# Decoder layer on one core: the cross attention's context rows and Wk Wq prepared inside the MLP, the last chunk turned back first, router biases loaded earlier

## The chip, the core and the metric

The kernel runs on one core of a Trainium2 chip. TensorE (PE) does the matmuls, VectorE (DVE), ScalarE (ACT) and GpSimd (POOL) the element-wise work, SyncE (SP) issues most DMAs. Each engine works through a queue of its own in program order; engines wait for each other by semaphores. The metric is the device time of one execution in microseconds (us), lower is better.

## What is computed

One decoder layer on 2048 tokens of 256 columns, in float32, each part with a residual and a layer norm. Cut to what matters here:

```python
x = layernorm(x + attn(x))            # decayed linear attention, then an MLP 256 -> 1024 -> 256
x = layernorm(x + xattn(x, context))  # context: 1601 rows of 256
x = layernorm(x + ffn(x))             # 8 experts, top 2

def xattn(slots, P, ...):
    Pn = rmsnorm(P, input_norm_w)
    k_proj, v_proj = Pn @ Wk.T, Pn @ Wv.T
    for _ in range(3):
        sn = rmsnorm(slots, slot_norm_w)
        scores = (sn @ Wq.T) @ k_proj.T * d ** -0.5
        attn = softmax(scores, axis=-2)                  # over the slots
        attn = attn / (sum(attn, axis=-1) + eps)
        slots = gru(attn @ v_proj, slots)

def ffn(x):                                              # router
    logits = x @ router_w + router_b + expert_bias
    # softmax, top 2, each token through its two experts
```

## The kernel before

The layer is a sequence of blocks; between two blocks all engines meet. Tokens are worked in NC = 4 chunks of CH = 512 columns, or NT = 16 tiles of P = 128 rows (TPC = 4 tiles in a chunk); the context in MT = 13 row tiles, the last with 65 rows. A column of 256 is DH = 2 halves. Products that need float32 accuracy are made from two parts each, a high part rounded to the fast format (`_hi`, a copy by ACT or POOL) and the rest (`_lo`, a subtraction by DVE or POOL), in three matmuls (`three_pass`, lines 74 to 78).

**`decay_attention_and_mlp`** makes the attention and the MLP, and ends with the layer norm of its result, turned into `sT` (columns on partitions). In the MLP loop over chunks c, PE makes 8 up-products of f (bank 6 or 7), ACT takes GELU (line 330) and its high part (335), DVE the low part `g_lo` (488); then PE makes the down-products of the chunk's 4 tiles, DVE adds them to the residual and normalises them (lines 496 to 505), and PE turns the normalised chunk (`turn_x1`, 588), which ACT copies to `sT` (`take_x1`, 306). ACT's GELU n waits until DVE has made the low part of n - 2 (`g_ok`); PE's up-product n waits for GELU n - 2 (`gelu_ok`). DVE's queue holds for each chunk: 8 low parts, 4 tiles, a chain of small operations (`rsqrt_steps`, 63 to 71, each waiting for the one before), 4 scalings; then the next chunk's low parts. POOL's residual additions (247, 248) lie in the MLP's first chunk. In the tail PE turns chunks 2 and 3. SP loads at the start, among others, `wk`, `wq`, `wv`, the turned context `cxT` and the norm weights (`early`), and stores each finished chunk.

**`prepare_context`** is a block of its own. Its work:

- PE makes Wk Wq (bank 0 and 1), which DVE scales to `wkq`; two broadcasts of the slots' norm factors (`norm.broadcast`); 8 key products (`keys`, 1450: wkq by cxT, 6 of 512 columns and 2 of 65), the other two broadcasts among them; and then `wi` = Wv by the GRU's weights (1457).
- ACT makes the high parts of the slots (`slots_hi`, 703), of the keys (1352), keeps the broadcasts in `rsB` (779), makes the context rows' 13 sums of squares (1364), and the high parts of `wh` (1373), of the context rows (1376, in two groups of 8 and 5 tiles) and of `wi` (1379).
- DVE makes the diagonals for the broadcasts (699), low parts of slots (707) and keys (1397), then waits for the 13 sums of squares, makes the rows' factors by the small chain, scales the 13 row tiles (1416), and makes the low parts of the rows' first group (1421) and of `wi` (1424), and the biases (1428 to 1430).
- POOL makes the low parts of `wh` (1337) and of the rows' second group (1339).
- SP loads the context rows `cx` (1.6 MB) and the GRU's weights when the block begins.

**`cross_attention`** then runs three iterations. In each, PE makes score products (m, c) of context tile m and slot chunk c; DVE scales each by `rsB` (1003, `scale(m, c)`); ACT takes the exponential; PE multiplies the weights by the rows; and a GRU updates the slots by chunk. At the end of an iteration SP writes the norm factors of chunks 0 to 2 to memory and loads them back spread over the partitions into `rsB` (`rs_in`); the last chunk's factors go another way (square sums by PE at 734, the chain by DVE from 742, a broadcast by PE). The first scaling of the next iteration, scale(0, 0), waits for all three loads. PE's order there: (0,0), (0,1), (0,2), (1,0), (1,1), square sums, (1,2), (0,3), broadcast. DVE's: scale(0,0), (0,1), low part of the last slots, scale(0,2), (1,0), the chain, and on. POOL adds the squares of the last chunk.

Behind the third iteration each chunk is turned back to rows (`turn_back`, 1161), added to the residual by DVE (955), normalised (`factors_of` by DVE, `apply` by ACT at 858), turned again (`turn_rows`, 1173) and multiplied by the router (`logits`, 1181); DVE takes the logits (`take_logits`, 965).

**`route`** loads the two bias vectors, adds them to the logits (1592, 1593), and finds for each token its experts and places. POOL makes constants meanwhile. SP loads, behind the biases, the experts' biases and 8 MB of `w2`. **`experts`** begins when those have landed: ACT's first high parts of `w1` (1794), DVE's low parts (1845), then the turned tokens (1839), then PE's first product.

## Time and profile before

| | |
|---|---|
| runs of the kernel | 1331.2, 1335.5, 1340.9 us; median 1335.5 |
| the profiled execution | 1336.2 us, of which the profile's span is 1334.4 |
| mean granted TensorE clock | 0.936 of 2.4 GHz |
| PE, DVE, ACT, POOL busy, share of the span | 88%, 66%, 47%, 19% |
| MLP (from its first up-product) | 90.6 to 203.0 us |
| preparation of the context | 210.4 to 248.2 us |
| three iterations | 248.7 to 946.8 us |
| last norm, router, experts, combination | 946.8 to 1334.4 us |

How to read the rows: in a timeline a row gives the start in us from the span's start, the duration in us, the engine, the line of the kernel, the operation, the tiles (out<-in), shapes and how many are merged. In brackets stands how long the engine had been idle before, and what ended the idle time. A group by line gives after the bar busy us and mean ns of one, then the idle time before them. PE is TensorE's matmuls, PEld its weight loads, SPq the DMA issues of SyncE. `x_psum`, `a_psum` are the PSUM banks. A table of stretches gives for each the length, then busy us of PE, PEld, DVE, ACT, POOL with the number of instructions in brackets, the granted clock as a share of 2.4 GHz, the DMA share and GB/s.

### The profile page before, as it was taken

How to read it: one execution, taken by the hardware profiler on the slowest of the kernel's cores; microseconds unless marked ns; L12 is line 12 of the kernel's file. 1: busy time of each engine (PE TensorE's matmuls, PEld its weight loads, DVE VectorE, ACT ScalarE, POOL GpSimd, SP SyncE). 2: the span in 40 equal slices, each digit the busy share in tenths (PEclk: the TensorE clock that was granted, in tenths of full speed). 3: DMA queues.
4: the chain of work that ended last, by engine and by line, in shares of the span. 5: the costliest groups of instructions: out<-in, count | busy, mean ns of one | idle time of the engine just before them, and what ended most of it. 6: DMA issues, size and time to landing. Idle time of an engine off the chain costs nothing. (4 is left out here: it accounts for less than half of the span.)

```text
span 1334.4 us, 18897 instructions
## 1 busy us (share of the span) xinstructions
PE 1176.1 (88%) x6332; PEld 981.9 (74%) x6332; DVE 884.1 (66%) x1863; ACT 621.1 (47%) x1057; POOL 251.2 (19%) x317
## 2 busy tenths in 40 slices
PE   6968997699999989999998999999628999999950
PEld 5437894478787867878786787778528999999950
DVE  4646545698745669874556987456466777777747
ACT  4335535354434334443433445334206777777733
POOL 3016000200000000000000000000035666666623
PEclk8869998899999999999999999999758999999985
DMA  7000003000010000001000000270081111111143
GB/s 275 1 0 10 23 17 112 1 0 1 0 28 5 17 9 0 1 0 32 1 17 9 0 1 0 63 285 32 32 285 41 46 38 43 47 43 43 40 150 126
DMA packets 43566, 62.57 MB, mean 47 GB/s; under 512 B 13102, under 2 KB 33264, under 8 KB 42608
## 3 DMA queue, kind: packets, MB, share of 16 engines
q1 hardware_dynamic: 37856, 47.35, 10.5%
q0 software_dynamic: 4416, 12.06, 3.0%
q10 hardware_dynamic: 1232, 2.36, 0.5%
q8 instruction: 36, 0.59, 0.2%
q14 instruction: 26, 0.21, 0.1%
HBM read 49.40 MB, written 12.36 MB: 46 GB/s over the span
## 5 line engine op out<-in xcount | busy, mean ns | idle before, releaser
L76 PE MATMUL x_psum<-x_sn_lo,x_kq_hi 128*128 128x512 f32 (+1 forms) x312 | 126.5, 405 | 17.8 <-PEq L1324 12.0
L76 PE MATMUL x_psum<-x_p_lo,x_v_hi 128*128 128x512 f32 (+1 forms) x312 | 125.9, 404 | 5.2 <-DVE x_p_lo L990 5.2
L77 PE MATMUL x_psum<-x_sn_hi,x_kq_lo 128*128 128x512 f32 (+1 forms) x312 | 124.8, 400 | 0.0
L78 PE MATMUL x_psum<-x_sn_hi,x_kq_hi 128*128 128x512 f32 (+1 forms) x312 | 124.4, 399 | 0.0
L77 PE MATMUL x_psum<-x_p_hi,x_v_lo 128*128 128x512 f32 (+1 forms) x312 | 123.0, 394 | 0.0
L78 PE MATMUL x_psum<-x_p_hi,x_v_hi 128*128 128x512 f32 (+1 forms) x312 | 123.0, 394 | 0.0
L899 ACT ACTIVATE x_e<-x_e,x_inv 128x1024 f32<-128x1024 f32 (+1 forms) x39 | 45.0, 1153 | 142.0 <-DVE x_inv L1009 142.0
L76 PE MATMUL e_bank<-e_w_lo,e_g_hi 128*128 128x256 f32 x368 | 107.6, 292 | 0.1
L76 PE MATMUL e_bank<-e_xT_lo,e_w_hi 128*128 128x256 f32 x368 | 105.1, 286 | 2.1 <-DVE e_xT_lo L1839 1.4
L78 PE MATMUL e_bank<-e_xT_hi,e_w_hi 128*128 128x256 f32 x368 | 104.8, 285 | 0.0
L77 PE MATMUL e_bank<-e_xT_hi,e_w_lo 128*128 128x256 f32 x368 | 104.8, 285 | 0.0
L77 PE MATMUL e_bank<-e_w_hi,e_g_lo 128*128 128x256 f32 x368 | 103.9, 282 | 0.0
L78 PE MATMUL e_bank<-e_w_hi,e_g_hi 128*128 128x256 f32 x368 | 103.8, 282 | 0.0
L726 POOL TENSOR_TENSOR x_E_rest<-x_E_rest 128x512 f32<-128x512 f32 x8 | 10.4, 1296 | 454.0 <-ACT x_E_rest L720 454.0
L1809 ACT ACTIVATE sT<-e_bank,b 128x256 f32<-128x256 f32 x184 | 76.9, 469 | 19.2 <-PE e_bank L78 19.2
L76 PEld LDWEIGHTS x_psum<-x_sn_lo,x_kq_hi 128*128 128x128 f32 (+1 forms) x312 | 58.6, 188 | 35.4 <-issue 12.4
L1853 DVE TENSOR_TENSOR e_w_lo<-w,e_w_hi 128x512 fp32r<-128x512 f32 x92 | 66.0, 718 | 27.4 <-issue 14.3
L1865 DVE TENSOR_TENSOR e_g_lo<-sT,e_g_hi 128x512 fp32r<-128x512 f32 x92 | 63.7, 692 | 28.1 <-ACT e_g_hi L1814 19.6
L76 PEld LDWEIGHTS x_psum<-x_p_lo,x_v_hi 128*128 128x128 f32 (+1 forms) x312 | 58.6, 188 | 24.3 <-DVE x_p_lo L990 9.4
L76 PEld LDWEIGHTS e_bank<-e_xT_lo,e_w_hi 128*128 128x128 f32 x368 | 71.4, 194 | 2.7 <-DVE e_xT_lo L1839 1.8
L76 PEld LDWEIGHTS e_bank<-e_w_lo,e_g_hi 128*128 128x128 f32 x368 | 70.1, 191 | 2.7 <-DVE e_w_lo L1853 0.4
L77 PEld LDWEIGHTS e_bank<-e_xT_hi,e_w_lo 128*128 128x128 f32 x368 | 71.4, 194 | 0.0
(392 smaller groups left out, 3132.3 us busy)
## 6 DMA issues: line engine op xcount, KB each, us to landing
w<-in_w SPq DMA_DIRECT2D x16, 1024.0 KB, 12.6
w<-scratch_results SPq DMA_DIRECT2D x8, 512.0 KB, 8.0
x_E_first<-scratch_row_inv SPq DMA_DIRECT2D x3, 1024.0 KB, 4.7
sT<-in_xT ACTq DMA_DIRECT2D x4, 512.0 KB, 12.4
a_x<-in_x SPq DMA_DIRECT2D x4, 512.0 KB, 8.3
scratch_x<-a_h SPq DMA_DIRECT2D x4, 512.0 KB, 2.7
w<-scratch_x SPq DMA_DIRECT2D x1, 2048.0 KB, 8.2
out<-w SPq DMA_DIRECT2D x4, 512.0 KB, 2.9
```

Source lines behind the costliest of these rows:

```text
L76: pe.matmul(out, w_hi, x_lo, start=start, stop=False)
L77: pe.matmul(out, w_lo, x_hi, start=False, stop=False)
L78: return pe.matmul(out, w_hi, x_hi, start=False, stop=stop)
L726: pool.tensor_tensor(sq[:, 0], sq[:, 0], sq[:, 1], ALU.add).then_inc(sum_ok, 1)
L899: act.activation(scores, scores, ACT.Exp, bias=inv[0:n, m, 0:1], accum_out=mx[0:n, m % 2, NC + half:NC + half + 1]).then_inc(exp_ok, 1)
L1809: act.activation(g32[f % 2][:, a], bank[1 + f % 2][:, a * SLOTS:(a + 1) * SLOTS], ACT.Gelu, bias=b1[:, bass.ds(ex * FT + (2 * f + a), 1)]) ...
L1853: v.tensor_tensor(w2_lo[:, 2 * f:2 * f + 2], w2[:, bass.ds(ex, 1), 2 * f:2 * f + 2].rearrange("p e c f -> p (e c) f"), w2_hi[:, 2 * f:2 * ...
L1865: v.tensor_tensor(g_lo[:, 2 * f:2 * f + 2], g32[f % 2], g_hi[:, 2 * f:2 * f + 2].bitcast(F32), ALU.subtract).then_inc(g_lo_ok, 1)
```

## The change

- The context rows, `wkq` and the rows' factors get places that lie in the MLP's memory, over buffers of the attention that are free by then. SP loads the rows once the attention's result `h2` is complete and POOL has cleared the last tile.
- ACT makes the 13 sums of squares behind chunk 1's last GELU; DVE makes the factors and scales the rows in place behind chunk 1's layer norm, ahead of chunk 2's low parts.
- PE makes Wk Wq between `turn_x1(2)` and `turn_x1(3)`; ACT, not DVE, scales it, between the two `take_x1`.
- In the preparation PE begins with a key product and puts the broadcasts between the first keys; ACT's and DVE's orders are written anew (the rows' high parts early, the last two keys late); POOL splits the rows before `wh`; the biases are made before the low part of `wi`; SP loads only the GRU's weights.
- In the iterations the first scaling waits for two slices of `rsB`; the third has a semaphore of its own, for which scale(0, 2) waits.
- `turn_back(3)` comes before `turn_rows(2)` and `logits(2)`.
- The router's two bias vectors are loaded at the start of the cross attention; `router_b` is added by `take_logits`, and `route` begins with one addition less and without its wait.

```diff
@@ decay_attention_and_mlp
+        context_at = -(-nc.sbuf_base // 32) * 32
+        for name, shape in (("cx", [P, MT, D]), ("wkq", [P, DH, D]), ("c_ss", [P, MT]), ("c_rs", [P, MT]), ("c_tmp", [P, MT])):
+            early[name] = nc.alloc_sbuf_tensor_at("y_" + name, shape, F32, offset=context_at)
+            context_at = -(-(context_at + math.prod(shape[1:]) * 4) // 32) * 32
...
+            sp.wait_ge(cx_zeroed, 1)
+            sp.dma_start(cx[:, 0:FULL], io["ctx"][0:FULL * P].rearrange("(t p) d -> p t d", p=P)).then_inc(ld_cx, 16)
+            sp.dma_start(cx[0:MROWS[-1], FULL], io["ctx"][FULL * P:]).then_inc(ld_cx, 16)
...
             pool.wait_ge(h2_sb, 2 * NC)
+            pool.memset(cx[:, FULL], 0.0).then_inc(cx_zeroed, 1)
             pool.wait_ge(up_mm, 2)
...
+                if c == 1:
+                    act.wait_ge(ld_cx, 32)
+                    for m in range(MT):
+                        if m >= 2:
+                            act.wait_ge(cx_squares, m - 1)
+                        act.activation(junk[:, m % 2], cx[:, m], ACT.Square, accum_out=c_ss[:, m:m + 1]).then_inc(cx_squares, 1)
             take_x1(NC - 2)
+            for h in range(DH):
+                act.wait_ge(wkq_mm, h + 1)
+                act.activation(wkq[:, h], bank[6 + h][:, 0:D], ACT.Copy, scale=early["cols"][:, h:h + 1])
             take_x1(NC - 1)
...
                 last.then_inc(x1_ok, 1)
+                if c == 1:
+                    v.wait_ge(cx_squares, MT)
+                    k.step(v.tensor_scalar(c_ss[:], c_ss[:], 1.0 / D, EPS_RMS, ALU.mult, ALU.add))
+                    rsqrt_steps(v, k, c_rs[:], c_ss[:], c_tmp[:])
+                    for m in range(MT):
+                        v.tensor_scalar(cx[:, m], cx[:, m], c_rs[:, m:m + 1], None, ALU.mult)
...
             turn_x1(NC - 2)
+            pe.wait_ge(gelu_ok, NC * FT)
+            pe.wait_ge(shared["ld_early"], 80)
+            for h in range(DH):
+                for j in range(DH):
+                    last = pe.matmul(bank[6 + h][:, 0:D], early["wk"][:, j, h * P:(h + 1) * P], early["wq"][:, j],
+                                     start=(j == 0), stop=(j == DH - 1))
+                last.then_inc(wkq_mm, 1)
             turn_x1(NC - 1)
@@ cross_attention
-                v.tensor_copy(shared["lg"][:, c * TPC:(c + 1) * TPC], bank[7][:, 0:TPC * NE].rearrange("p (t e) -> p t e", e=NE)).then_inc(lg_ok, 1)
+                v.tensor_tensor(shared["lg"][:, c * TPC:(c + 1) * TPC], bank[7][:, 0:TPC * NE].rearrange("p (t e) -> p t e", e=NE),
+                                bc(rb[:, 0], 1, TPC), ALU.add).then_inc(lg_ok, 1)
...
                     if c == 0 and m == 0 and it > 0:
-                        v.wait_ge(rs_in, 16 * it * (NC - 1))
+                        v.wait_ge(rs_in, 16 * it * 2)
+                    if c == 2 and m == 0 and it > 0:
+                        v.wait_ge(rs_last_in, 16 * it)
...
+            sp.dma_start(rb[:, 0], io["router_b"].partition_broadcast(P)).then_inc(ld_r, 16)
+            sp.dma_start(rb[:, 1], io["expert_bias"].partition_broadcast(P)).then_inc(ld_r, 16)
...
+            turn_back(NC - 1)
             turn_rows(NC - 2)
             logits(NC - 2)
-            turn_back(NC - 1)
             turn_rows(NC - 1)
             logits(NC - 1)
@@ prepare_context: POOL
+            pool.wait_ge(v_hi_ok, 2)
+            pool.tensor_tensor(v_lo[:, VG[1]], v32[:, VG[1]], v_hi[:, VG[1]].bitcast(F32), ALU.subtract).then_inc(wh_lo_ok, 1)
             pool.wait_ge(wh_hi_ok, 1)
             pool.tensor_tensor(wh_lo[:], whT[:], wh_hi[:].bitcast(F32), ALU.subtract).then_inc(wh_lo_ok, 1)
-            pool.wait_ge(v_hi_ok, 2)
-            pool.tensor_tensor(v_lo[:, VG[1]], v32[:, VG[1]], v_hi[:, VG[1]].bitcast(F32), ALU.subtract).then_inc(wh_lo_ok, 1)
@@ prepare_context: ACT (order after)
+            slots_hi(act, 0)
             keys_hi(0)
             norm.keep(act, 0, 0)
+            slots_hi(act, 1)
             keys_hi(1)
             norm.keep(act, 1, 1)
+            keys_hi(2)
+            keys_hi(3)
             slots_hi(act, 2)
             norm.keep(act, 2, 2)
+            rows_hi(0)
+            keys_hi(4)
+            keys_hi(5)
             slots_hi(act, 3)
             norm.keep(act, 3, 3)
+            rows_hi(1)
             act.wait_ge(ld_g, 48)
             act.activation(wh_hi[:], whT[:], ACT.Copy).then_inc(wh_hi_ok, 1)
+            for i in range(6, len(keys)):
+                keys_hi(i)
@@ prepare_context: DVE
-            v.memset(cx[:, FULL], 0.0).then_inc(zeroed, 1)
             norm.spread(v, slot_rs, 0, 0)
             norm.spread(v, slot_rs, 1, 1)
-            v.wait_ge(ld_early, 80)
-            for h in range(DH):
-                v.wait_ge(wkq_mm, h + 1)
-                v.tensor_scalar(wkq[:, h], bank[h][:, 0:D], cols[:, h:h + 1], None, ALU.mult).then_inc(wkq_ok, 1)
+            k.mark(v.tensor_scalar(rs16[:], rs[:], float(D) ** -0.5, None, ALU.mult))
...
+            keys_lo(3)
             slots_lo(v, 2, 2)
-            keys_lo(3)
+            keys_lo(4)
+            keys_lo(5)
             slots_lo(v, 3, 3)
-            v.wait_ge(squares, MT)
-            k.step(v.tensor_scalar(ss[:], ss[:], 1.0 / D, EPS_RMS, ALU.mult, ALU.add))
-            rsqrt_steps(v, k, rs[:], ss[:], tmp[:])
-            for m in range(MT):
-                v.tensor_scalar(v32[:, m], cx[:, m], rs[:, m:m + 1], None, ALU.mult).then_inc(v32_ok, 1)
-            k.step(v.tensor_scalar(rs16[:], rs[:], float(D) ** -0.5, None, ALU.mult))
...
+            v.wait_ge(ld_g, 48)
+            k.mark(v.tensor_tensor(bias[:, 0:2 * DH], bi[:, 0:2 * DH], bi[:, 3 * DH:5 * DH], ALU.add))
@@ prepare_context: PE
-            norm.broadcast(pe, 0, 0)
-            norm.broadcast(pe, 1, 1)
-            pe.wait_ge(wkq_ok, DH)
             for i, (h, c) in enumerate(keys):
-                if i == 4 or i == 6:
-                    norm.broadcast(pe, i // 2, i // 2)
+                if i in (1, 2, 4, 6):
+                    g = (1, 2, 4, 6).index(i)
+                    norm.broadcast(pe, g, g)
@@ route
-            sp.dma_start(rb[:, 0], io["router_b"].partition_broadcast(P)).then_inc(ld_r, 16)
-            sp.dma_start(rb[:, 1], io["expert_bias"].partition_broadcast(P)).then_inc(ld_r, 16)
...
-            v.wait_ge(ld_r, 32)
-            k.step(v.tensor_tensor(lg[:], lg[:], bc(rb[:, 0], 1, NT), ALU.add))
             k.step(v.tensor_tensor(lg[:], lg[:], bc(rb[:, 1], 1, NT), ALU.add))
```

## Rows read from the trace of the kernel before

**Rows 1.** The page's first part: an engine's busy us, share of the span, instructions

```profile
PE 1176.1 (88%) x6332; PEld 981.9 (74%) x6332; DVE 884.1 (66%) x1863; ACT 621.1 (47%) x1057; POOL 251.2 (19%) x317
```

**Rows 2.** Timeline, edge of MLP chunks 1 and 2: start, us, engine, line, operation

```profile
154.36 0.69 ACT L330 ACTIVATE a_g<-a_psum,a_small 128x512 f32<-128x512 f32 x1 [12.15 <-PE a_psum L78]
...
157.85 1.29 DVE L488 TENSOR_TENSOR a_g_lo<-a_g,a_g_hi 128x512 fp32r<-128x512 f32 x2
...
158.63 0.69 ACT L330 ACTIVATE a_g<-a_psum,a_small 128x512 f32<-128x512 f32 x1 [1.56 <-DVE a_g_lo L488]
...
159.37 0.50 PE L76 MATMUL a_psum<-a_hT_lo,a_w_hi 128*128 128x512 f32 x1 [0.97 <-ACT a_g L330]
```

**Rows 3.** Groups by line, 208 to 260 us: busy us, mean ns of one, idle before

```profile
L1364 ACT ACTIVATE y_junk<-y_cx 128x256 f32<-128x256 f32 x13 | 5.2, 409 | 0.0
...
L1339 POOL TENSOR_TENSOR x_v_lo<-y_v,x_v_hi 128x1280 fp32r<-128x1280 f32 x1 | 3.8, 3835 | 7.0 <-ACT x_v_hi L1376 7.0
...
L1416 DVE TENSOR_SCALAR y_v<-y_cx,y_rs 128x256 f32<-128x256 f32 x13 | 3.5, 344 | 0.0
...
L1337 POOL TENSOR_TENSOR x_wh_lo<-y_whT,x_wh_hi 128x1536 fp32r<-128x1536 f32 x1 | 3.4, 3424 | 110.4 <-ACT x_wh_hi L1373 110.4
...
L1421 DVE TENSOR_TENSOR x_v_lo<-y_v,x_v_hi 128x2048 fp32r<-128x2048 f32 x1 | 2.3, 2292 | 0.1
...
L1424 DVE SCALAR_TENSOR_TENSOR x_wi_lo<-x_psum,y_cols,x_wi_hi 128x512 fp32r<-128x512 f32 (+1 forms) x4 | 2.2, 610 | 0.0
```

**Rows 4.** Busy us by stretch: PE, PEld, DVE, ACT, POOL, granted clock, DMA, GB/s

```profile
210.40:248.50 38.10, 24.21 (x64) 12.81 (x64) 27.38 (x65) 21.54 (x49) 7.26 (x2) 0.86 0.25 85
...
248.50:252.00 3.50, 3.25 (x8) 2.60 (x9) 0.53 (x2) 1.28 (x1) 0.00 (x0) 0.50 0.07 9
...
482.00:484.00 2.00, 2.00 (x6) 1.58 (x5) 1.57 (x5) 0.00 (x0) 0.00 (x0) 0.50 0.03 8
```

**Rows 5.** Timeline of DVE in the preparation

```profile
231.85 0.16 DVE L1413 TENSOR_SCALAR y_ss<-y_ss 128x13 f32<-128x13 f32 x1
...
233.92 3.37 DVE L70 TENSOR_TENSOR y_tmp<-y_tmp,y_ss 128x13 f32<-128x13 f32 x1
...
248.07 0.15 DVE L1430 COPY x_bias<-y_bi 128x2 f32<-128x2 f32 x1
```

**Rows 6.** Timeline of PE, end of the MLP and preparation

```profile
207.24 1.59 PE L588 MATMUL a_psum<-ident,a_h 128*128 128x128 f32 x8 [4.27 <-DVE a_h L505]
...
215.94 7.03 PE L1450 MATMUL x_psum<-y_cxT,y_wkq 128*128 128x512 f32 x16
```

**Rows 7.** Timeline of ACT, DVE and PE at the start of the second iteration

```profile
478.67 1.04 ACT L703 ACTIVATE x_sn_hi<-sT 128x1024 fp32r<-128x1024 f32 x1
...
479.58 0.75 DVE L1003 CUSTOM_DVE_ANT_0 x_e<-x_psum,x_rsB,x_rs 128x512 f32<-128x512 f32 x1 [1.91 <-DMA x_rsB<-scratch_slot_inv]
...
480.39 0.56 PE L76 MATMUL x_psum<-x_sn_lo,x_kq_hi 128*128 128x512 f32 x1 [2.23 <-DVE x_mx L1003]
...
485.82 0.16 DVE L742 TENSOR_SCALAR x_st<-x_psum 128x4 f32<-128x4 f32 x1 [1.94 <-PE x_psum L734]
```

**Rows 8.** Timeline of DVE and PE behind the last iteration

```profile
946.10 0.69 DVE L1102 TENSOR_TENSOR sT<-sT,x_E_rest 128x512 f32<-128x512 f32 x1
...
946.94 1.06 PE L1173 MATMUL x_psum<-ident,x_acc 128*128 128x128 f32 x8 [3.88 <-ACT x_acc L858]
...
953.38 1.48 DVE L955 TENSOR_TENSOR x_acc<-x_psum,x_acc 128x512 f32<-128x512 f32 x2 [6.59 <-PE x_psum L1161]
```

**Rows 9.** Timeline, routing and start of the experts

```profile
969.07 0.42 SPq L1553 DMA_DIRECT2D b<-in_b_cols  x1
...
971.17 0.29 DVE L1592 TENSOR_TENSOR lg<-lg,r_rb 128x128 f32<-128x128 f32 x1 [3.26 <-DMA r_rb<-in_expert_bias]
...
1000.97 1.15 ACT L1794 ACTIVATE e_w_hi<-w 128x512 fp32r x2 [28.19 <-DMA w<-in_w]
...
1006.28 0.58 PE L76 MATMUL e_bank<-e_xT_lo,e_w_hi 128*128 128x256 f32 x1 [1.41 <-DVE e_xT_lo L1839]
```

78 lines of the change are left out of this document (27 added, 51 removed).

## The prediction

> **What bounds the kernel now.** I read the page first: PE is busy 88% of the span, so a microsecond that PE loses is lost unless another engine had been late anyway, and what can be gained lies in the stretches where PE waits [rows 1]. The page's chain of the work that ended last covers only the last 40 us, so I went to the timeline of each engine around every edit, and to the clock and busy time by stretch.
>
> In the MLP, PE runs from chunk to chunk almost without a gap. The reader is to see what the gap of 0.97 us at 159.37 hangs on: PE's fifth up-product of chunk 2 waits for ACT's third GELU (158.63), and that waits for DVE's first `g_lo` of the chunk (157.85), which stands in DVE's queue behind the layer norm of chunk 1. ACT, in contrast, had been idle 12.15 us before its first GELU of the chunk [rows 2]. So at the edge between two chunks DVE has no slack at all and ACT has a lot.
>
> The preparation of the context runs from 210.4 to the end of the DVE copies at 248.22: 37.8 us. PE works 24.2 of it, DVE 27.4, ACT 21.5 [rows 4, 5]. The end is DVE's: it waits for its own square sums, scales 13 row tiles, and only then come the split of the rows and of `wi`.
>
> **The change, part by part** (plus is slower).
>
> *Squares and loading in the MLP.* ACT's 13 squares cost 5.2 us [rows 3] and come behind chunk 1's last GELU, in the 12.15 us of idle: 7 us stay, so zero. The context rows are asked for once `h2` is complete, before the first up-product, and are needed two chunks of products later; SP's next job, the first x1 store, is much later too, and POOL's memset stands in front of a wait for PE: zero.
>
> *Scaling in the MLP.* DVE gets 12 small chained operations and 13 scalings right behind the norm of chunk 1, ahead of the first `g_lo` of chunk 2. The small ones follow each other every 0.207 us (ten from 231.85 to 233.92), so 12 cost 2.5 us [rows 5]; the 13 scalings cost 3.5 [rows 3]. The `g_lo` at 157.85 comes 6.0 us later, the GELU too, and PE stands from 158.40 to about 165.3: +6.0, nothing hides it, since PE could already run only four up-products ahead. After such a pause PE's clock is low: in the first 3.5 us after the pause before 248.5 the granted clock is 0.50, which is 1.2 GHz of 2.4 [rows 4], and those 3.5 us do 1.75 us of work. I take +1.7 (bounds 0 and 2). PE then bounds the chunk again, so it is not won back. Together **+7.7** (6.0 to 8.0).
>
> *Wk Wq in the MLP's tail.* The eight instructions of 256 columns cost 1.7 us at the rate of the keys (16 of 512 in 7.03), 3.4 at the low clock, and PE is idle 4.27 us there, before it turns the last chunk at 207.24 [rows 6]; ACT's two copies also lie there. Zero; without this cover at most what runs over, under 1 us.
>
> *The preparation.* Gone are the Wk Wq products and DVE's two scalings of them, the squares, the chain and the row scalings. I laid the new order out from the block's start B, each step as long as its row of before. PE: a key product of four instructions takes 1.7 us at the full clock (16 in 7.03, four keys) [rows 6], twice that in the first 3.5 us; with the four broadcasts the sixth key is ready at B+14.6. ACT: high halves of slots and keys, copies and the two high halves of the rows follow one another and end at B+18.4; `wh_hi` ends at B+19.8, the last two keys at B+20.4. ACT's total work of 21.5 minus the squares [rows 3, 4] says the same from the other side: 16.3 less the 2 for `wi_hi` is 14.3, and it waits about 5 for its first keys. PE has the `wi` products (8 of 512 columns and 8 of 256, 5.3 at the same rate) done by B+22.6. What is late next is DVE and POOL. POOL splits its rows from B+18.4: 1280 columns at the rate of its 1536 in 3.42 [rows 3] are 2.85, to B+21.3. Then DVE's 2.13 (2.29 [rows 3], less the overlap) and POOL's 3.4 for `wh_lo` are both ready. They exclude each other: in before, a DVE operation of 13 columns took 3.37 us at 233.92, exactly while POOL was splitting `wh` [rows 5]; and POOL's own 1280 columns took 3.84 instead of 2.85 beside DVE's split [rows 3]. So they queue, in either order: B+21.3 + 2.1 + 3.4 = B+26.8, and then DVE's bias operations (0.6, the first has two SBUF inputs and queues too) and `wi_lo` (2.2 [rows 3]): B+29.5. Against 37.8 that is **-8.3**. If they never met the end would be B+25.5, gain 12.3; if the order of ACT costs two further microseconds the gain is 6.
>
> The Trainium skill (SBUF — State Buffer, section "SBUF: two separate sides") says that a DVE instruction with two SBUF inputs and a GpSimd instruction that reads SBUF take the shared ports as a lock, for the whole instruction. The trace agrees (3.37 us for 13 columns). By it DVE and POOL queue in the new order; with no such rule the total would be some 4 us lower.
>
> *The split wait at an iteration's start.* DVE's first scaling waits 1.91 us for the third slice of `rsB`, until 479.58, and PE 2.23 behind it [rows 7]; PE even falls to the low clock (0.50 from 482 to 484 [rows 4]). The new wait needs two slices, long there. The third is needed by scale(0, 2), which comes after two scalings (0.67 each from 477.67) and the low half of the last slots, which needs ACT's high half of 478.67 to 479.71: 480.9, past the landing at 479.6. So no new wait. PE runs products (1, 0) and (1, 1) from 478.4 instead of 480.39, 2.0 earlier, at full clock, which is 1.4 more; the square sums reach DVE at 482.3 instead of 485.82 [rows 7]: -3.5. There are two such boundaries: **-7.0**. Bounds: the waits alone, -3.8 (if PE's clock falls all the same), and somewhat more than 7 where the slice lands later, since all of the wait goes.
>
> *Last chunk turned back first.* Before, PE's order was rows of chunk 2, logits of chunk 2 and only then the last chunk; DVE was idle 6.59 us until 953.38. The slots are ready when DVE ends at 946.8, and PE starts 8 transposes in 1.06 us at 946.94 [rows 8]. In the new order these are the last chunk's: DVE starts at 947.5. Everything to the end of this stage hangs on that norm: **-5.9** (bounds: 5.2, if half of a low clock is met there, and the idle 6.59). Chunk 2's rows and logits move back 1.1 us and end by 954, before ACT has applied the last norm: zero.
>
> *Router biases.* DVE no longer waits 3.26 us and has one addition less (0.3), but POOL's constants bind it again after 2.7. Routing ends 2.7 earlier. The experts however start when the last expert weights land, 1000.97; ACT waited 28.19 for them [rows 9]. SP's first job behind the two bias loads is at 969.07, so that without them it is some 0.9 earlier (DVE had ended the stage before at 967.9), and DVE's four splits of `w1` then stand ahead of `xT_lo`, which lay before 1006.28 with ACT's copy still 1.3 behind; this queue allows 2.1. **-1.9** (bounds 0, if the gather lands no sooner, and -2.7). The two loads go to SP's queue at the start of the iterations, ahead of a wait for the first iteration's row sums: zero.
>
> The Trainium skill (DMA: Bandwidth & Descriptors, section "Queues, rings and completion order") has each DMA engine take turns between its queues, packet by packet. No row shows gather and weights together. By that rule an earlier gather shares with the weights and is not stuck behind them; if it were stuck, the gain would be the 0.9 alone.
>
> Sum: +7.7 - 8.3 - 7.0 - 5.9 - 1.9 = -15.4. The profiled execution took 1336.2 (span 1334.4 and 1.8 around it): 1320.8. The median of the runs is 0.7 below it: I predict **1320**.
>
> **Rivals.**
> 1. *Small gains.* PE's clock falls at both boundaries (-3.8), the preparation gains 6, the router nothing or 0.9: +8 - 6 - 3.8 - 5.2 - 0.5 = -7.5, 1328. For it: a pause of 2.2 us sufficed for the low clock at 480 [rows 4, 7], and a pause of about 1.9 remains ahead of the broadcast. Against it: there the square sums still come 2 us earlier.
> 2. *DVE and POOL do not meet, or the block opens at full clock*: 12.3 from the preparation, +6.5 in the MLP: -20.6, 1315. For it: the tail of the MLP now has PE work in its pause. Against: 3.37 us at 233.92 [rows 5].
> 3. *Slower.* PE does not get its full clock back after the 6.9 us pause in chunk 2. From 159.37 to the pause that ends at 207.24 [rows 2, 6] there are 42.6 us of dense work; all of it at 1.2 GHz costs 42.6 more in the place of 1.7: +25.5, 1361. It decides from 58 us of time at the low level (29 us lost: 15.4 eaten up, 13.4 to pass 1%). Against: after 248.5 the low level lasted 3.5 us [rows 4].
> 4. *The change does not do what it says*: the context rows land late and ACT's squares hold its GELUs. They have two chunks of products to land 1.6 MB; I give it nothing of its own.
>
> **How the numbers follow.** Forecast 0.50, rival 1 0.28, rival 2 0.18, rival 3 0.04. The forecast's own range, from its bounds, is 1316 to 1325. To leave out no more than 2 in 10 the range takes in rival 1 and most of rival 2: 1313 to 1329. A measurement of this kernel tells about 1% from no change, 13.4 us, so 1322.1 is the line. Of the forecast 0.44 lies below it, and all of rival 2; of rival 1 nothing: faster 0.62. Slower by over 1% is rival 3: 0.04. The rest, 0.34, is within 1%.
>
> **What would show it.** In chunk 2 of the MLP one PE wait for ACT of 6.9 us in the place of 0.97, with the clock at 0.50 behind it; a preparation of 29.5 us with DVE's split or POOL's visibly stretched; no DMA wait of DVE at the first scaling, and the square sums 3.5 us earlier; DVE's wait for the turned last chunk below 1 us; a wait for the weights still ahead of the experts. I am wrong in the sum if DVE's insertion costs PE less than 5 (some slack I don't see), or if the preparation ends in ACT rather than in DVE and POOL.

## The result, and the profile after

| | before | changed |
|---|---|---|
| median of 12 runs | 1333.8 us (1331.2 to 1341.9) | 1324.9 us (1321.4 to 1330.0) |
| the profiled execution, and its span | 1336.2, 1334.4 us | 1321.4, 1319.7 us |
| PE busy | 1176.1 us | 1176.3 us |

The ratio is 0.9927 with a 95% interval of 0.9903 to 0.9951: 9.7 us less (6.5 to 12.9). The time lies in the range, and even at the edge of the forecast's own range (1316 to 1325); the gain however was forecast as 15.4 us, and 62% of the chance had been put on a gain of over 1%, which this isn't.

The spans of the two profiled executions stand 14.7 us apart, more than the medians (8.9). So the first thing to do is to cut both into stages at points that both traces have: first up-product of the MLP; first high part of the slots (ACT); first score product; the last GRU addition of each iteration (DVE); DVE's last take of the logits; first expert product. Each stage is the difference of two starts.

| stage, us | before | changed | difference | forecast |
|---|---|---|---|---|
| attention (untouched) | 90.6 | 86.1 | -4.5 | 0 |
| MLP | 119.8 | 127.3 | +7.5 | +7.7 |
| preparation | 38.3 | 30.7 | -7.6 | -8.3 |
| first iteration | 228.2 | 230.7 | +2.4 | 0 |
| second and third | 469.1 | 463.8 | -5.3 | -7.0 |
| last norm | 21.6 | 16.4 | -5.2 | -5.9 |
| routing | 38.6 | 36.4 | -2.1 | -1.9 |
| experts (untouched) | 328.1 | 328.2 | +0.1 | 0 |

The attention has the same code in both, and its 4.5 us are PE's clock alone: the granted clock falls there at other moments. Over the 14 profiled kernels of this study the attention takes 86.0 to 95.7 us. Without the two untouched stages the change is worth -10.3 in this pair of traces, which agrees with the ratio of the runs.

**MLP.** Timeline of DVE, ACT and PE in the changed kernel, where [rows 2] showed the edge between chunks 1 and 2: start, us, engine, line, operation, and in brackets the idle time and what ended it.

```profile
152.88 0.17 DVE L529 TENSOR_SCALAR y_c_ss<-y_c_ss 128x13 f32<-128x13 f32 x1
...
155.38 3.50 DVE L532 TENSOR_SCALAR y_cx<-y_cx,y_c_rs 128x256 f32<-128x256 f32 x13
158.80 1.28 DVE L508 TENSOR_TENSOR a_g_lo<-a_g,a_g_hi 128x512 fp32r<-128x512 f32 x2
...
159.57 0.69 ACT L341 ACTIVATE a_g<-a_psum,a_small 128x512 f32<-128x512 f32 x1 [7.47 <-DVE a_g_lo L508]
...
160.31 0.79 PE L76 MATMUL a_psum<-a_hT_lo,a_w_hi 128*128 128x512 f32 x1 [6.88 <-ACT a_g L341]
```

The chain and the 13 scalings fill DVE from 152.88 to 158.8, the third GELU waits for the low part behind them, and PE stands 6.88 us in the place of 0.97.

**Preparation.** Timeline of DVE and POOL, the counterpart of [rows 5].

```profile
233.01 2.90 POOL L1366 TENSOR_TENSOR x_v_lo<-y_cx,x_v_hi 128x1280 fp32r<-128x1280 f32 x1 [114.48 <-ACT x_v_hi L1381]
...
234.95 3.10 DVE L1439 TENSOR_TENSOR x_v_lo<-y_cx,x_v_hi 128x2048 fp32r<-128x2048 f32 x1
...
235.87 5.46 POOL L1368 TENSOR_TENSOR x_wh_lo<-y_whT,x_wh_hi 128x1536 fp32r<-128x1536 f32 x1
...
237.98 3.37 DVE L1441 TENSOR_TENSOR x_bias<-y_bi 128x4 f32<-128x4 f32 x1
...
241.41 2.18 DVE L1446 SCALAR_TENSOR_TENSOR x_wi_lo<-x_psum,y_cols,x_wi_hi 128x512 fp32r<-128x512 f32 x4
```

POOL's split of 1280 columns ends at 235.91, and DVE's of 2048, begun at 234.95, takes 3.10 us instead of 2.29 in before [rows 3]. Then POOL takes 5.46 us for what took 3.42, the rest of DVE's split (235.9 to 238.0) and then its own 3.4 us, and DVE's addition of four columns takes 3.37 us, to 241.35, just past the end of POOL's split at 241.33. So each of the two engines in turn is stretched to the other's end, three times in a row, and `wi_lo` comes last.

**Clock.** Busy us of PE, PEld, DVE, ACT, POOL by stretch, then the granted clock, the DMA share and GB/s, the counterpart of [rows 4].

```profile
213.40:244.00 30.60, 23.15 (x56) 11.08 (x56) 21.60 (x37) 16.82 (x23) 8.32 (x2) 0.83 0.14 52
244.10:247.60 3.50, 3.47 (x8) 2.81 (x9) 0.76 (x2) 1.28 (x1) 0.00 (x0) 0.50 0.11 12
247.60:249.60 2.00, 2.00 (x6) 1.53 (x5) 0.23 (x2) 0.00 (x0) 0.00 (x0) 0.50 0.00 0
485.60:488.60 3.00, 3.00 (x9) 2.32 (x8) 1.40 (x5) 2.97 (x4) 0.00 (x0) 0.50 0.00 0
```

Behind the first score product (244.13) the clock is at 0.50 (1.2 GHz) until 250.1, that is for 6.0 us, where it had been 3.2 in before (248.75 to 252.0). It is at 0.50 once more behind the boundary between two iterations, now from 485.6, behind the broadcast; there it lasts 3.4 us. Such a stretch at 0.50 in the middle of PE's work is called a low spell from here on.

**Boundary, last norm, routing.** Timeline of DVE, PE and ACT, the counterpart of [rows 7 to 9].

```profile
475.42 0.74 DVE L1040 CUSTOM_DVE_ANT_0 x_e<-x_psum,x_rsB,x_rs 128x512 f32<-128x512 f32 x1
...
480.32 0.15 DVE L775 TENSOR_SCALAR x_st<-x_psum 128x4 f32<-128x4 f32 x1
...
484.80 0.50 PE L807 MATMUL x_psum<-x_diag_parts,x_ones_r 128*128 128x512 f32 x1 [1.87 <-DVE x_diag_parts L792]
...
939.54 1.90 PE L1200 MATMUL x_psum<-ident,sT 128*128 128x128 f32 x8 [3.99 <-DVE sT L1139]
...
940.69 1.48 DVE L989 TENSOR_TENSOR x_acc<-x_psum,x_acc 128x512 f32<-128x512 f32 x2 [1.41 <-PE x_psum L1200]
...
955.04 0.19 DVE L999 TENSOR_TENSOR lg<-x_psum,rb 128x32 f32<-128x32 f32 x1 [8.34 <-PE x_psum L1220]
955.55 0.29 DVE L1599 TENSOR_TENSOR lg<-lg,rb 128x128 f32<-128x128 f32 x1 [0.32 <-PEq L683]
...
984.83 2.19 ACT L1800 ACTIVATE e_w_hi<-w 128x512 fp32r x4 [27.62 <-DMA w<-in_w]
...
988.96 1.12 PE L1902 MATMUL e_bank<-ident,sT 128*128 128x128 f32 x4 [7.90 <-DMA sT<-scratch_x,e_tokens]
991.49 0.58 PE L76 MATMUL e_bank<-e_xT_lo,e_w_hi 128*128 128x256 f32 x1 [1.41 <-DVE e_xT_lo L1845]
```

The first scaling (475.42) has no wait. The square sums (480.32) come 5.51 us behind the last addition of the slots, 8.84 in before. The last chunk is turned first, and DVE waits 1.41 us for it instead of 6.59. Routing starts 0.3 us after its block, and the wait that ends last ahead of the experts is PE's for the gathered tokens (988.96); the weights have been there since 984.83. The last of the eight weight loads lands 28.9 us behind DVE's last take, and the gather's first DMA is issued at 29.1, so that whether the two share the DMA engines, as the prediction assumes, stays open.

### The profile page after: what moved, and what is told of

Read it like the earlier page. It is cut to its first block and busy times, and to the rows that moved or that the text cites. A ratio compares the mean times of both kernels' runs of the same rounds, so it can differ in the third digit from the quotient of the medians.

```text
span 1319.7 us, 18896 instructions
## 1 busy us (share of the span) xinstructions
PE 1176.3 (89%) x6332; PEld 983.3 (75%) x6332; DVE 883.1 (67%) x1859; ACT 622.7 (47%) x1059; POOL 253.2 (19%) x318
## 3 DMA queue, kind: packets, MB, share of 16 engines
q1 hardware_dynamic: 37856, 47.35, 10.3%
```

## The experiments

All stages of all kernels, in us, one profile each; the ratio is to the kernel before, of the timed ones. The first part undoes or isolates parts of the change, the second alters one thing in the changed kernel, the third combines what gained.

| kernel | attn | MLP | prep | it. 1 | it. 2 | it. 3 | norm | route | ratio (95%) |
|---|---|---|---|---|---|---|---|---|---|
| before | 90.6 | 119.8 | 38.3 | 228.2 | 232.3 | 236.8 | 21.6 | 38.6 | |
| changed | 86.1 | 127.3 | 30.7 | 230.7 | 229.0 | 234.8 | 16.4 | 36.4 | 0.9927 (0.9903, 0.9951) |
| p_late | 86.0 | 119.3 | 38.1 | 228.1 | 229.5 | 232.7 | 15.8 | 36.2 | 0.9918 (0.9886, 0.9951) |
| p_early | 86.0 | 127.2 | 30.7 | 230.7 | 232.0 | 237.5 | 21.6 | 38.7 | 1.0022 (0.9991, 1.0053) |
| u_one_wait | 86.3 | 127.6 | 30.8 | 231.1 | 232.1 | 237.4 | 15.8 | 36.0 | |
| u_back_last | 86.0 | 127.3 | 30.7 | 230.7 | 229.0 | 234.3 | 21.9 | 35.9 | |
| u_router | 86.4 | 127.3 | 30.7 | 231.0 | 229.0 | 234.3 | 16.3 | 38.6 | |
| e_spread | 95.7 | 119.2 | 29.6 | 229.5 | 229.5 | 236.0 | 16.5 | 36.2 | 0.983 (0.979, 0.9869) |
| e_bias_last | 86.7 | 127.3 | 28.6 | 229.9 | 229.0 | 232.8 | 16.5 | 36.3 | 0.9897 (0.9849, 0.9946) |
| e_warm | 87.3 | 127.4 | 30.7 | 227.7 | 229.5 | 232.8 | 15.8 | 36.1 | |
| e_warm_tail | 87.6 | 128.9 | 27.7 | 229.9 | 229.0 | 234.3 | 16.4 | 36.2 | |
| e_warm_bound | 90.7 | 127.5 | 30.8 | 230.7 | 228.7 | 233.9 | 15.8 | 36.2 | |
| c_spread_bias | 90.6 | 119.6 | 27.7 | 228.9 | 229.0 | 233.7 | 15.9 | 36.4 | 0.98 (0.976, 0.9841) |
| c_all | 91.2 | 119.6 | 25.7 | 226.9 | 227.5 | 234.3 | 15.8 | 36.2 | 0.9782 (0.9748, 0.9817) |

### The two halves of the change: p_late and p_early

p_late is the kernel before with the split wait, `turn_back(NC - 1)` first and the router biases; p_early is the changed kernel with these three undone.

> The kernel before with only the three late parts of the change (the split wait for rsB, the last chunk turned back first, the router biases); the MLP and the preparation are those of before. Theory A (the stages of the two profiles add up): these parts account for -3.3 and -2.0 at the two boundaries, -5.2 behind the third iteration and -2.1 in routing, together -12.6 us, and the early half of the change is worth about nothing (+7.5 in the MLP, -7.6 in the preparation), so this kernel stands at 0.9905 of before and at or somewhat below the whole change. Theory B (the early half brings a gain that the late parts need, for example because the clock is better when the iterations begin earlier): it stands at 0.995 or above. The MLP's first pause in chunk 2 is 0.97 us again, the preparation 38.3 us.

> The whole change without its three late parts: only the context rows and Wk Wq in the MLP and the new order of the preparation. Theory A: +7.5 in the MLP and -7.6 in the preparation, and 0 to +2.5 in the first iteration if its longer low clock belongs to the change: within 0 to +2.5 us of before, ratio 0.999 to 1.002. Theory B (the early half is a gain of its own): ratio 0.997 or below. The profile shows the pause of 6.9 us in chunk 2 and a preparation of 30.7 us, and whether PE's clock stays low for 3.3 us after the first score product, as in before, or 5.2, as in the changed kernel.

Measured: 0.9918 and 1.0022. Theory A holds: p_early's interval leaves out theory B's 0.997, and p_late's only just reaches its 0.995. The product of the two is 0.9940, the whole change 0.9927. More than half of the diff, all that moves work into the MLP, brings nothing that can be measured: what the preparation gets back (-7.6) the MLP has paid (+7.5), and the first iteration takes 2.4 more on top.

### Each late part undone: u_one_wait, u_back_last, u_router

```diff
@@ u_one_wait
-                        v.wait_ge(rs_in, 16 * it * 2)
-                    if c == 2 and m == 0 and it > 0:
-                        v.wait_ge(rs_last_in, 16 * it)
+                        v.wait_ge(rs_in, 16 * it * (NC - 1))
...
@@ u_back_last
-            turn_back(NC - 1)
             turn_rows(NC - 2)
             logits(NC - 2)
+            turn_back(NC - 1)
@@ u_router: SP and DVE in routing; the two loads and the addition are gone from the cross attention
+            sp.dma_start(rb[:, 0], io["router_b"].partition_broadcast(P)).then_inc(ld_r, 16)
+            sp.dma_start(rb[:, 1], io["expert_bias"].partition_broadcast(P)).then_inc(ld_r, 16)
...
+            v.wait_ge(ld_r, 32)
+            k.step(v.tensor_tensor(lg[:], lg[:], bc(rb[:, 0], 1, NT), ALU.add))
```

> The changed kernel with one wait for all three slices of rsB again. Theory A (the gain at a boundary is the DMA wait alone, 1.9 to 2.3 us, since a low spell of PE's clock is paid either way): the square sums reach DVE 8.8 and 9.1 us after the last addition instead of 5.5, a low spell stands at the wait instead of behind the broadcast, and the second iteration takes 231 us, the third 236 to 237. A further low spell about 150 us behind the boundary (634 and 632 us in the two kernels with one wait so far, and in one of seven with the split wait) would add 1.7: 232.3. Theory B (the split saves the spell too, 3.5 at each boundary): 232.5 and 238.3.

Timeline of DVE in u_one_wait, the scaling and the square sums:

```profile
478.76 0.75 DVE L1038 CUSTOM_DVE_ANT_0 x_e<-x_psum,x_rsB,x_rs 128x512 f32<-128x512 f32 x1 [2.27 <-DMA x_rsB<-scratch_slot_inv]
...
484.91 0.16 DVE L775 TENSOR_SCALAR x_st<-x_psum 128x4 f32<-128x4 f32 x1 [1.61 <-PE x_psum L767]
```

The wait is back with 2.27 us, and the square sums come 9.11 us behind the last addition (475.80) instead of 5.5. The second and the third iteration take 232.1 and 237.4 us, 3.1 more each than in u_router, which has the split wait. Theory A had 232.3 for the second with a further low spell, and one stands at 633 us; theory B's 232.5 is too near to that to tell them apart. The third, 237.4, lies between A's 237 and B's 238.3, with a further spell at 865.

What tells them apart is a comparison at equal spells. The third iteration with a spell at the boundary and one late in the iteration takes 237.5 and 237.4 us with one wait (p_early, u_one_wait) and 236.0 with the split (e_spread); with the boundary's spell alone 236.8 (before) and 234.3 to 234.8 (changed, u_back_last, u_router, e_warm_tail). So the split is worth 1.4 to 2.5 us at this boundary, which is about the wait (2.27 us there in before), as in theory A. But a spell is not paid either way: the one-wait kernels have one at each of their 6 boundaries, the nine kernels with the split and no small products there at 14 of 18.

Over all kernels the second and third iteration together take 469.1, 469.4 and 469.5 us with one wait (before, p_early, u_one_wait) and 461.8 to 465.5, in the middle 463.3, with the split wait (those nine). That is 6.1 us, not 7.0. But the one-wait kernels have 3, 4 and 4 low spells in these two iterations and the nine others 1 to 3, 1.8 on average. At 1.7 us for a spell (half of 3.4) fewer spells make some 3 of the 6.1 us, by estimate, and the waits the other half.

> The changed kernel with the last chunk turned back behind the rows and logits of chunk 2 again. Expected by the stages: 21.6 us from the last addition to the last logits instead of 15.8 to 16.5, DVE's wait for the turned chunk 6.6 us instead of 1.4; routing unchanged at 36.2. If the order gained only what the clock gave (a rival reading of 16.5 against 15.8), less than 1 us.

Timeline of DVE in u_back_last: the residual addition behind the turned last chunk.

```profile
945.41 1.48 DVE L989 TENSOR_TENSOR x_acc<-x_psum,x_acc 128x512 f32<-128x512 f32 x2 [6.81 <-PE x_psum L1200]
```

As expected: 21.9 us and 6.81 us of wait. The order is worth 5.2 to 6.0 us (21.6 or 21.9 against 16.4 or 15.8).

> The changed kernel with the router's biases loaded and added in routing again. Theory A (routing is bound by the weights' landing in before and by the gather in the changed kernel): from the last logits to the first expert product 38.6 us instead of 36.2 to 36.4, the first low parts of w1 and the turned tokens next to each other as in before. Theory B (POOL's constants bind routing's start in both): DVE's first comparison waits the same 3.3 us but the stage is below 37. The last norm's stage stays at 16.5 or lower.

Timeline of DVE, ACT and PE in u_router: first addition, first high part of `w1`, turned tokens, first product.

```profile
958.49 0.29 DVE L1599 TENSOR_TENSOR lg<-lg,r_rb 128x128 f32<-128x128 f32 x1 [3.26 <-DMA r_rb<-in_expert_bias]
...
988.32 2.19 ACT L1801 ACTIVATE e_w_hi<-w 128x512 fp32r x4 [28.22 <-DMA w<-in_w]
...
991.12 1.11 PE L1903 MATMUL e_bank<-ident,sT 128*128 128x128 f32 x4 [7.33 <-DMA sT<-scratch_x,e_tokens]
993.64 0.58 PE L76 MATMUL e_bank<-e_xT_lo,e_w_hi 128*128 128x256 f32 x1 [1.41 <-DVE e_xT_lo L1846]
```

38.6 us, so 2.2 more, as A says. But what binds is not what changes most. From DVE's last take (955.04 in both kernels) the weights land after 33.3 us here and 29.8 in the changed kernel, the gathered tokens after 36.1 and 33.9, and the first product follows the tokens by 2.5 in both. The gather is last in both, and in before too (1003.75 - 967.72 = 36.0). My expectation had given before to the weights; that was wrong.

### The place of the scalings: e_spread

```diff
@@ DVE, MLP, chunk c
-                if c == 1:
-                    v.wait_ge(cx_squares, MT)
...
+                if c == 2:
+                    v.wait_ge(cx_squares, MT)
+                    k.step(v.tensor_scalar(c_ss[:], c_ss[:], 1.0 / D, EPS_RMS, ALU.mult, ALU.add))
+                    rsqrt_steps(v, k, c_rs[:], c_ss[:], c_tmp[:])
                 for t in range(c * TPC, (c + 1) * TPC):
...
                     k.step(v.bn_aggr(mv[:, t], stats[:, t]))
+                    if c == 2:
+                        for m in range((0, 4, 8, MT, MT)[t % TPC], (4, 8, MT, MT, MT)[t % TPC]):
+                            v.tensor_scalar(cx[:, m], cx[:, m], c_rs[:, m:m + 1], None, ALU.mult)
```

> The changed kernel with DVE's chain for the rows' factors put behind the eighth low part of chunk 2, where DVE waits for the first down-product, and the 13 scalings behind the statistics of that chunk's tiles 0, 1 and 2 (4, 4 and 5), where DVE waits 1.8 us for each next tile. Theory A (the place in DVE's queue costs the 7.5 us, not the work): PE's pause in chunk 2 is 0.97 us again, its clock stays at the full level behind it, and the kernel gains 7.5 us: ratio to before 0.987, against 0.9927 of the whole change. Theory B (DVE has no slack for 6 us anywhere in the MLP): the pause moves to chunk 3 with 3 to 6 us, and the gain is below 3 us.

Timeline of PE and DVE in e_spread: PE's two gaps of chunks 2 and 3, and the scalings between them.

```profile
163.87 0.50 PE L76 MATMUL a_psum<-a_hT_lo,a_w_hi 128*128 128x512 f32 x1 [0.97 <-ACT a_g L341]
...
176.16 1.14 DVE L526 TENSOR_SCALAR y_cx<-y_cx,y_c_rs 128x256 f32<-128x256 f32 x4
...
178.35 1.14 DVE L526 TENSOR_SCALAR y_cx<-y_cx,y_c_rs 128x256 f32<-128x256 f32 x4
...
180.54 1.41 DVE L526 TENSOR_SCALAR y_cx<-y_cx,y_c_rs 128x256 f32<-128x256 f32 x5
...
188.39 0.50 PE L76 MATMUL a_psum<-a_hT_lo,a_w_hi 128*128 128x512 f32 x1 [0.92 <-ACT a_g L341]
```

Theory A holds: the same 25 operations cost nothing where DVE waits for PE's down-products. The pause is 0.97 us, that of chunk 3 0.92, the MLP takes 119.2 us (8.1 less than in the changed kernel), and the ratio falls to 0.983. The preparation, 1.1 us shorter, had not been expected: its clock is at the full level from 218.6 here, 3.7 us after its first product, and in the changed kernel from 219.4, 5.9 us after it (0.67 on average over 217.2 to 220.5). The 2.2 us more at half speed are the 1.1.

### The shared ports: e_bias_last

```diff
@@ DVE, preparation
-            k.mark(v.tensor_tensor(bias[:, 0:2 * DH], bi[:, 0:2 * DH], bi[:, 3 * DH:5 * DH], ALU.add))
...
             for i, (h, n0, n) in enumerate(gru):
...
+            k.mark(v.tensor_copy(bias[:, 2 * DH:3 * DH], bi[:, 2 * DH:3 * DH]))
+            k.mark(v.tensor_copy(bias[:, 3 * DH:], bi[:, 5 * DH:]))
+            k.step(v.tensor_tensor(bias[:, 0:2 * DH], bi[:, 0:2 * DH], bi[:, 3 * DH:5 * DH], ALU.add))
```

> The changed kernel with DVE's three small bias operations behind the low parts of wi, the addition last. Theory A (a DVE instruction with two inputs in SBUF and a POOL instruction exclude each other, one that reads PSUM and SBUF doesn't wait): wi_lo runs beside POOL's split of wh, from about 3.1 us after DVE began on the rows, the addition no longer takes 3.4 us, POOL's split ends as before at 241.3 - 213.4 = 27.9 us after the block's start, and the preparation ends 2 us earlier, 28.6 us instead of 30.7. Theory B (DVE waits for POOL in any form): the preparation stays within 0.3 of 30.7, and the first operation of wi_lo shows the 3.4 us. The whole time changes by at most 2 us, 0.15%, which the stage shows and the total can't.

Timeline of POOL and DVE in e_bias_last:

```profile
236.46 5.47 POOL L1368 TENSOR_TENSOR x_wh_lo<-y_whT,x_wh_hi 128x1536 fp32r<-128x1536 f32 x1
...
238.57 2.18 DVE L1442 SCALAR_TENSOR_TENSOR x_wi_lo<-x_psum,y_cols,x_wi_hi 128x512 fp32r<-128x512 f32 x4
240.68 1.28 DVE L1446 COPY x_bias<-y_bi 128x2 f32<-128x2 f32 x1
...
241.94 0.15 DVE L1448 TENSOR_TENSOR x_bias<-y_bi 128x4 f32<-128x4 f32 x1
```

`wi_lo`, which reads PSUM and SBUF, runs in 2.18 us in the middle of POOL's split. The copy of two columns behind it takes 1.28 us instead of 0.15 and ends at 241.96, POOL's split at 241.93: it was stretched too, and the expectation had not said so. The preparation takes 28.6 us, the number of theory A to the tenth. The Trainium skill (SBUF — State Buffer, section "Who interferes with whom") has it this way: a DVE instruction with at most one SBUF input, outside the two-port modes, doesn't contend; one with two SBUF inputs does, with a GpSimd instruction that reads SBUF; and a copy can, when it enters a two-port mode. The rows agree with the first (2.18 us) and the second (3.37 us in the changed kernel); the copy's 1.28 us fit the third, but no row shows in which mode it ran.

### PE kept busy in its pauses: e_warm, e_warm_tail, e_warm_bound

Small products of 128 columns, into a PSUM bank that nobody reads then; they compute nothing of the result.

```diff
@@ e_warm: PE, end of the preparation
+            pe.wait_ge(kq_lo_ok, len(keys))
+            for i in range(26):
+                pe.matmul(bank[0][:, 0:P], wv[:, 0, 0:P], wiT[:, 0, 0:P], start=True, stop=True)
@@ e_warm_tail: PE, end of the MLP
+            pe.wait_ge(z_ok, NT - 1)
+            for i in range(11):
+                pe.matmul(bank[0][:, 0:P], ident[:], ident[:], start=True, stop=True)
             turn_x1(NC - 1)
+            for i in range(7):
+                pe.matmul(bank[0][:, 0:P], ident[:], ident[:], start=True, stop=True)
@@ e_warm_bound: PE, iterations
                     if (m, c) == (0, 3) and it > 0:
+                        pe.wait_ge(rsB_ok, NC + it - 2)
+                        for i in range(7):
+                            pe.matmul(bank[7][:, 0:P], ident[:], ident[:], start=True, stop=True)
                         norm.broadcast(pe, NC + it - 1, LAST)
```

> The changed kernel with 26 small products of PE (128 columns, into a bank nobody reads then) behind the wi products of the preparation, which fill most of PE's idle time there; nothing else. So far the first iteration, from its first score product to the last addition of its GRU, took 228.1 and 228.2 us with the preparation of before and 229.5 to 230.7 in four kernels with the new one, with a granted clock of 0.50 for 5 us behind the first score product instead of 3.3, and in three of them for 3.4 us at about 400 as well. Theory A (this is the clock alone, by how PE's pause lies): with PE busy until some 1.3 us before the first score product the clock there is at or near the full level, and the first iteration takes 226 to 228 us. Theory B (the loss belongs to something else in the new order, such as buffers or loads): it stays at 229.5 or above. The preparation stays at 30.7.

Timeline of PE in e_warm, the small products and the first score product, and the stretch behind it:

```profile
238.42 5.97 PE L1473 MATMUL x_psum<-y_wiT,y_wv 128*128 128x128 f32 x52
245.42 0.47 PE L76 MATMUL x_psum<-x_sn_lo,x_kq_hi 128*128 128x512 f32 x1 [1.03 <-PEq L1356]
```

```profile
245.42:249.40 3.98, 3.98 (x17) 3.27 (x18) 1.74 (x5) 1.25 (x1) 0.00 (x0) 1.00 0.07 6
```

With a pause of 1.03 us instead of 6.82 the clock is at the full level from the first score product on, and the first iteration takes 227.7 us instead of 230.7. Theory A holds: the iteration's loss was PE's clock. The sizes fit: 6.0 us less at half speed are 3.0 us.

One low spell of 3.4 us at 398, behind a pause of 1.1 us, stays. It is there in all nine kernels that have the 6.9 us pause in chunk 2, and in none of the five without it (before, p_late, e_spread, c_spread_bias, c_all), though all 14 have the pause of 1.1 us. What ties the two together, 240 us apart, no run shows. Nor does this pause decide alone: it comes in each iteration, where PE waits for ACT (`x_E_rest`) behind the last row products. Timeline of PE in the changed kernel at this pause, in the first and in the second iteration, and the stretches behind:

```profile
400.10 0.65 PE L76 MATMUL x_psum<-x_sn_lo,x_wh_hi 128*128 128x512 f32 x1 [1.11 <-ACT x_E_rest L914]
...
630.31 0.50 PE L76 MATMUL x_psum<-x_sn_lo,x_wh_hi 128*128 128x512 f32 x1 [1.11 <-ACT x_E_rest L914]
```

```profile
400.30:403.70 3.40, 3.40 (x9) 2.63 (x9) 1.86 (x3) 3.38 (x4) 0.00 (x0) 0.50 0.01 2
630.31:634.00 3.69, 3.63 (x14) 2.66 (x15) 1.90 (x3) 3.67 (x4) 0.00 (x0) 1.00 0.02 4
```

The same pause, to the hundredth, is followed by a spell in the one place and not in the other.

> The changed kernel with 11 small products of PE ahead of the turning of the last chunk in the MLP's tail and 7 behind it, so that PE has hardly a pause between the MLP and the preparation. In the changed kernel the clock is low from 212 to 220 us and the first four instructions of a key take 3.75 us instead of 1.7. Theory A (the preparation's start hangs on PE's clock through the first keys): the preparation takes 28 to 29.5 us instead of 30.7. Theory B (it is set by ACT's and DVE's own work): 30.3 to 30.7. The MLP stays at 127.3.

Timeline of PE in e_warm_tail: small products, the turned last chunk, small products, the first key.

```profile
210.65 2.62 PE L672 MATMUL a_psum<-ident 128*128 128x128 f32 x22
213.35 1.06 PE L614 MATMUL a_psum<-ident,a_h 128*128 128x128 f32 x8
214.25 1.73 PE L675 MATMUL a_psum<-ident 128*128 128x128 f32 x14
216.56 1.95 PE L1466 MATMUL x_psum<-y_cxT,y_wkq 128*128 128x512 f32 x4 [0.58 <-PEq L85]
```

The first four instructions of a key take 1.95 us instead of 3.75 and the preparation 27.7 instead of 30.7, 0.3 below theory A's range. In the changed kernel the clock is low for the stage's first 6.0 us, and half of that is the 3.0. (The MLP's 128.9 comes from its first chunk, where the clock is low for 6.8 us from 102.3, in the changed kernel for 3.4 from 96.5; the last chunk is turned 5.3 us behind the third in both kernels, so the small products hold nothing up.)

> The changed kernel with 7 small products of PE in the pause of 1.87 us ahead of the last chunk's broadcast, at both boundaries between iterations. In the changed kernel the wait for the third slice is gone, but PE's clock is at the low level for 3.4 us behind this broadcast (485 to 489 and 714 to 718 us), as it was behind the DMA wait in before (480 to 484 and 712 to 717). Theory A (the low spell has moved from the one pause to the other and still costs 1.7 us each): no spell behind the broadcast, the second iteration takes 227.3 us instead of 229.0 and the third 232.8 instead of 234.8. Theory B (the spells come by chance and not from this pause): spells at 485 or 715 as before.

Timeline of PE in e_warm_bound at the broadcast, and the stretch behind it:

```profile
489.65 0.50 PE L807 MATMUL x_psum<-x_diag_parts,x_ones_r 128*128 128x512 f32 x1 [0.28 <-DVE x_diag_parts L792]
```

```profile
490.40:493.40 3.00, 3.00 (x14) 2.41 (x14) 1.45 (x5) 2.96 (x4) 0.00 (x0) 1.00 0.00 0
```

Theory A holds for the place: no low spell behind either broadcast, nor behind the two of c_all, which has the same small products. One kernel alone would not show it, since at the second boundary four of the nine kernels with the 1.87 us pause have no spell either; 0 of 4 against 14 of 18 does. The gain is mostly lost again: spells of 3.4 us stand at 634 and 863 us, both behind the 1.1 us pause, and the stages take 228.7 and 233.9, against 227.3 and 232.8 as expected. With no spell at all the second iteration takes 227.5 (c_all).

### The combinations: c_spread_bias and c_all

c_spread_bias has the edits of e_spread and e_bias_last, c_all those two and the three with small products, 17 instead of 26 at the end of the preparation.

> Both edits that gained: DVE's scalings spread over chunk 2's waits, and the bias operations behind wi_lo. By the stages so far: MLP 119.2, preparation 27.5 (29.6 with the spread alone, 28.6 with the bias alone, 30.7 with neither), so 11.3 us below the changed kernel's stages; ratio to before 0.984. If the two gains don't add up (a second bound of the preparation at 28.6), ratio 0.985 and a preparation of 28.6.

> All edits that gained, in one kernel: the scalings spread over chunk 2's waits, the bias operations last, and PE kept busy in three pauses (the MLP's tail, the end of the preparation with 17 small products, the pause ahead of the last chunk's broadcast). If the stages add up: MLP 119.3, preparation 25.7 (30.7 less 3.0 for the tail's products and 2.1 for the bias operations), first iteration 227.7, second 227.0, third 232.8, last norm 15.9, routing 36.2; with 86 to 92 us for the attention 1298 to 1304 us of span, ratio to before 0.976. If keeping PE busy only moves the low spells to the next pause, the preparation and the iterations stay where the kernel with two edits had them (27.7, 228.9, 229.0) and the ratio is 0.980 as there.

c_spread_bias has a preparation of 27.7 and a ratio of 0.980: the gains add up. c_all has the preparation at 25.7, the first iteration at 226.9 and the second at 227.5 as the stages say; the third has a low spell at 845 us, again behind the 1.1 us pause, and takes 234.3 instead of 232.8. Its median is 1305.3 us over six runs, a ratio of 0.9782 (0.9748 to 0.9817), against 0.976 by the sum; the interval holds both this and c_spread_bias's 0.980, so that what the small products give is shown by the stages and not by the total. It beats both kernels: 28 us below before, 20 below the changed one.

## Why the prediction was right where it was, and where its sum failed

**What held.** DVE's insertion in the MLP: +7.5 for +7.7, a pause of 6.88 us for 6.9, with the clock at the low level behind it; e_spread shows that it was the place. The wait at the boundary: the square sums come 3.3 and 3.6 us earlier, for 3.5. The last norm: -5.2, its lower bound, "if half of a low clock is met there": PE's turning took 1.90 us instead of 1.06 at the clock it met at 939.54. The queue of DVE and POOL in the preparation, three waits long. The squares, the loads and Wk Wq cost nothing: e_spread has them all, and its MLP takes 119.2 us, no more than before's 119.8. Rival 2 fell with the stretched rows, rival 3 with a clock that was back at its full level 4.4 us behind the pause in chunk 2, rival 4 with squares that ran when due (ACT was idle 6.93 us more behind them).

**The step that failed** is that the clock was only counted where I looked. The sum has +1.7 for it in the MLP, 3.5 us at the preparation's start as in before, and nothing in the stages after, as though a pause of another length would leave the clock of the next stage as it was. It didn't, at three places, each time against the forecast:

- The first iteration had no term at all. It lost 2.4 us: its opening is at the low level for 6.0 us instead of 3.2, and a spell stands at 400. e_warm gives 3.0 back with PE busy ahead of it.
- At the boundaries the term was -3.5 each, of which 1.4 for "at full clock". The products there do run at full clock, but the spell moved behind the broadcast, where PE pauses 1.87 us; I had named that pause in rival 1, as a reason against the gain, and not priced it in the forecast. The small products of e_warm_bound take this spell away. In the pair of profiles the term is -5.3, and that is nearer to -7.0 than its mechanism earned: the third iteration has the same spell in both and gains 2.0, the second gains 3.3, of which 1.2 to 1.7 us, by estimate, are before's further spell at 634, far from the boundary. At equal spells a boundary gains 1.4 to 2.5 us, so that the wait was right and the 1.4 for the clock was not.
- The preparation was laid out with 3.5 us of low clock at its start. It was low for 6.0 us, 2.5 more, which is 1.2 us of work, and POOL's rows start 1.2 us later than laid out (B+19.6 instead of B+18.4); e_warm_tail shows that PE's clock in the first keys is worth 3.0 us of this stage. The bias operations made up for part: 0.6 had been laid out for them behind POOL's split, but the addition ended with that split (B+27.9). The end is B+30.2 for B+29.5.

Together 2.4 + 1.7 + 0.7 + 0.7 (last norm), less 0.4 in the MLP and routing, are the 5.1 us between -15.4 and -10.3.

**Right number, wrong cause**: routing. The term of -1.9 came from the weights' landing; measured -2.1, but the tokens' gather is last in before and after. What moved is the gather's issue (2.7 us earlier behind DVE's last take), less half a microsecond more from issue to landing. The weights landed 3.5 us earlier and not 0.9: the first of the eight loads 1.4 earlier, and the others mostly 2.7 us behind each other instead of 3.0. The same difference stands between p_early and u_router, which have the bias loads ahead of the weights, and p_late and u_back_last, which have not; why isn't shown.

**The chances.** Rival 1 ("small gains", -7.5) lay nearer to the ratio's -9.7 than the forecast did, and its mechanism, the clock at the boundaries, was part of what happened. 28% for it was too little, since in the trace of before a low spell stands behind both boundary pauses (2.23 and 2.60 us) and a third behind one of 1.1 us. That the time lies within the forecast's own range (1324.9, its edge is 1325) is in part luck: with the split wait there are on average 1.9 low spells fewer in the second and third iteration, and no term of the sum stands for that.

## What to carry to other kernels

Work moved under other work costs nothing only at a place where the engine that takes it waits for the one that sets the end: the same 25 DVE operations cost 7.5 us ahead of the next chunk's low parts and nothing between the tiles of a chunk. When a stage gets shorter, price the pauses of PE that it leaves, ahead of the next stage also; small products into an unused bank removed the low clock there (3.0 us in one place, 3.0 in another). And split two traces into stages at common points before explaining their difference: here an untouched stage made a third of it.
